# A grouped convolution in row tiles, on x in order of time

## What is computed

```python
def _L0_cond_ref(x, c, weight, c_weight, bias):   # 4 groups of 32 channels, 9 taps, padding 4
    out = lax.conv_general_dilated(x, weight, window_strides=(1,), padding=[(4, 4)],
              dimension_numbers=('NCH', 'OIH', 'NCH'), feature_group_count=4)
    return out + jnp.einsum('nd,od->no', c, c_weight)[:, :, None] + bias[None, :, None]

def _L1_cond_ref(x, embedding, W0, b0, W1, b1, W2, b2, weight, bias_k):
    h = gelu(embedding @ W0 + b0);  h = gelu(h @ W1 + b1)
    att = softmax(h @ W2 + b2)                              # 8 weights for each sample
    agg_w = jnp.einsum('bk,koi->boi', att, weight[..., 0])  # a 128x128 matrix for each sample
    return jnp.einsum('boi,bih->boh', agg_w, x) + (att @ bias_k)[:, :, None]

x = x + _L0_cond_ref(x, cond_128, ...)
x = x + _L1_cond_ref(x, cond_128, ...)
```

## Time and profile before

| | us |
|---|---|
| median of 3 runs | 840.06 |
| the profiled execution | 839.29 |
| its span, first to last instruction | 837.4 |
| TensorE busy in it | 766.2 |
| ACT busy | 637.2 |
| POOL busy | 552.1 |
| DVE busy | 410.1 |

### The profile page before, as it was taken

How to read it: one execution, slowest core, us unless ns; L and a number is a source line. 1 busy time by engine, 2 the same in 40 slices (tenths; PEclk the granted TensorE clock), 3 DMA queues, 4 the chain that set the end, 5 groups by cost and what they waited for, 6 DMA issues and landing times.

```text
span 837.4 us, 15303 instructions
## 1 busy us (share of the span) xinstructions
PE 766.2 (92%) x5424; PEld 600.9 (72%) x5424; DVE 410.1 (49%) x299; ACT 637.2 (76%) x291; POOL 552.1 (66%) x596
## 2 busy tenths in 40 slices
PE   2659998999999999999999999999999999999994
PEld 2547776777777777777777777777777777777773
DVE  6662455445445555444555445445554444554430
ACT  7766886888778877878786787888777868866554
POOL 3289686667778767767876666668667566866620
PEclk9988999999999999999999999999999999999997
DMA  5778999999999999999999999999999999987643
GB/s 194 206 230 263 309 317 292 305 326 306 325 314 330 313 313 308 318 301 306 329 318 306 297 312 312 319 331 332 305 314 300 284 305 327 319 257 247 220 164 126
DMA packets 91011, 242.90 MB, mean 290 GB/s; under 512 B 15914, under 2 KB 58482, under 8 KB 74610
## 3 DMA queue, kind: packets, MB, share of 16 engines
q1 hardware_dynamic: 90994, 242.67, 91.5%
HBM read 101.57 MB, written 75.50 MB: 211 GB/s over the span
## 4 chain that ended last, share of the span: by engine, by line
SPq 46%; PE 20%; DMA 20%; ACT 6%; issue 6%; POOL 1%; DVE 0%; POOLq 0%
SPq L240 34%; DMA mix_dram<-mix_parts 16%; PE ps L366 12%; SPq L264 9%; PE ps L383 8%; DMA mix_rep<-mix_dram 3%; ACT z_out L448 3%; SPq L272 2%; ACT x_ph L429 1%; ACT x_cv L452 1%; DMA x_in<-in_x_dram 1%; ACT z_out L452 0%; SPq L214 0%; PE ps L353 0%; POOL mix_prod L646 0%
## 5 line engine op out<-in xcount | busy, mean ns | idle before, releaser
L448 ACT ACTIVATE z_out<-ps,par 128x2048 f32<-128x2048 f32 x64 | 253.3, 3957 | 143.0 <-PE ps L383 143.0
L515 DVE TENSOR_TENSOR y_lo<-ps,y_hi 128x1024 fp32r<-128x1024 f32 x128 | 156.4, 1222 | 305.9 <-ACT y_hi L438 305.9
L429 ACT ACTIVATE x_ph<-x_in 128x2048 f32<-128x2048 f32 x63 | 246.5, 3914 | 0.0
L366 PE MATMUL ps<-x_hi,cw_hi 128*128 128x512 f32 x768 | 228.6, 406 | 0.3 <-DVE y_lo L515 0.3
L366 PE MATMUL ps<-x_hi,cw_lo 128*128 128x512 f32 x768 | 221.3, 397 | 0.0
L366 PE MATMUL ps<-x_lo,cw_hi 128*128 128x512 f32 x768 | 220.2, 395 | 0.0
L383 PE MATMUL ps<-y_hi,mix_rep 32*128 32x512 f32 x2048 | 179.7, 418 | 41.2 <-DMA mix_rep<-mix_dram 32.8
L366 PEld LDWEIGHTS ps<-x_hi,cw_hi 128*128 128x128 f32 x768 | 141.1, 191 | 52.2 <-issue 15.0
L366 PEld LDWEIGHTS ps<-x_hi,cw_lo 128*128 128x128 f32 x768 | 145.9, 190 | 33.9
L366 PEld LDWEIGHTS ps<-x_lo,cw_hi 128*128 128x128 f32 x768 | 145.4, 189 | 33.7
L438 ACT ACTIVATE y_hi<-ps 128x1024 fp32r<-128x1024 f32 x128 | 131.0, 1023 | 47.3 <-PE ps L366 47.3
(11 more groups left out here) (69 smaller groups left out, 87.8 us busy)
## 6 DMA issues: line engine op xcount, KB each, us to landing
x_in<-in_x_dram SPq DMA_DIRECT2D x64, 1024.0 KB, 6.2
out_dram<-z_out SPq DMA_DIRECT2D x64, 1024.0 KB, 5.9
x_cv<-x_ph SPq DMA_DIRECT2D x496, 128.0 KB, 3.8
mix_rep<-mix_dram SPq DMA_DIRECT2D x256, 128.0 KB, 4.0
mix_dram<-mix_parts SPq DMA_DIRECT2D x64, 128.0 KB, 2.7
mixw_nat<-in_L_cond_weight_dram SPq DMA_DIRECT2D x1, 512.0 KB
x_cv<-x_ph SPq DMA_DIRECT2D x8, 64.0 KB, 4.2
z_out<-in_L_cond_weight_dram SPq DMA_DIRECT2D x1, 144.0 KB, 2.2
```

The source lines that it names most:

```text
L366: mm = pe.matmul(y_ps[:, g, :], w[:, g, b, :], xx[buf(s)][:, g, b:b + N], start=n == 0, stop=n == len(terms) - 1)
L429: nc.scalar.activation(x_ph[pair_buf(s)][:, :, buf(s), :], x_in[buf(s)][:, :].rearrange("c (n q) -> c q n", q=PH), ACT.Copy).then_inc(x_sp ...
L448: nc.scalar.activation(z_out[buf(s)][:, :].rearrange("c (n q) -> c q n", q=PH), z_ps[:, :, :], ACT.Identity, bias=par[s[1]][:, NK:NK + 1]) ...
L515: nc.vector.tensor_tensor(y_lo[buf(s)][:, y_halves[h], :], y_ps[:, y_halves[h], :], y_hi[buf(s)][:, y_halves[h], :].bitcast(F32), ALU.subt ...
```

## The change

The convolution also runs in row tiles. Tile g is group g: its 32 rows are the group's 32 channels, as x lies in SBUF anyway, and its 128 weight columns are again 4 phases by 32 outputs. There are 12 offsets in time (`M`), nine taps for each of four phases, so a tile makes 12 by 3 terms = 36 matmuls (`CONV`), and a round of four tiles takes the place of one matmul of 128 rows. The moving operand for offset m is column n's point 4n+m: TensorE reads every fourth element of `x_hi` or `x_lo`, a step of 16 bytes. `x_ph`, `x_cv`, `split_phases` and `move_x` are gone; DVE splits `x_in` directly.

The tiles are staggered: tile t is `LAG` = 4 steps behind tile t-1. A slot has 48 steps, 36 of the convolution and 12 of the previous sample's mix. ACT and DVE take y bank by bank, ACT takes z two banks at a time, reading the two banks in turn and writing pairs of neighbours. The loads run 3 samples ahead (7 before), SP's order in a slot is load, store_mix, store, load_mix, and the small network's matmuls stand between the first sample's steps. The identity that adds x to the convolution is now added to the taps by a matmul.

```diff
+        def x_at(tile, rows, m):
+            return tile[rows, :].rearrange("p (n q) -> p n q", q=PH)[:, m // PH:m // PH + N, m % PH]
...
-            def conv(s):
...
-                        mm = pe.matmul(y_ps[:, g, :], w[:, g, b, :], xx[buf(s)][:, g, b:b + N],
-                                       start=n == 0, stop=n == len(terms) - 1)
...
+            between = {4: (turn_cond,), 10: (first_layer, turn_mixw), 20: (second_layer,), 28: (third_layer,),
+                       32: (context_mixed,), 44: (attention,)}
+            def conv_step(s, g, i):
...
+                rows = slice(Q * g, Q * g + Q)
+                if i == 0:
+                    if g == 0:
+                        pe.wait_ge(x_lo_made, done(s))
+                    at_least(pe, y_lo_made, done(s, G, lag=-2) + g + 1)
+                m, term = i // 3, i % 3
+                w, xx = ((cw_hi, x_hi), (cw_lo, x_hi), (cw_hi, x_lo))[term]
+                mm = pe.matmul(y_ps[:, g, :], w[rows, m, :], x_at(xx[buf(s)], rows, m),
+                               start=i == 0, stop=i == CONV - 1)
...
             def slot(s):
-                conv(s)
-                mix(after(s, -1))
+                for i in range(STEPS):
...
+                    for t in range(PH):
+                        if i >= LAG * t:
+                            step(s, t, i - LAG * t)
+                        else:
+                            step(after(s, -1), t, i - LAG * t + STEPS)
...
-            def take_z(s):
+            def take_z(s, h):
...
+                pair = slice(2 * h, 2 * h + 2)
+                nc.scalar.activation(z_out[buf(s)][:, :].rearrange("c (n q) -> c n q", q=PH)[:, :, pair], z_ps[:, pair, :].rearrange("c q n -> c n q"),
+                                     ACT.Identity, bias=par[s[1]][:, NK:NK + 1]).then_inc(z_read, 1)
...
             def slot(s):
-                if is_sample(s, 0):
-                    finish_table()
-                else:
-                    split_x(after(s, 1))
-                rest_y(s, 0)
-                rest_y(s, 1)
+                if not is_sample(s, 0):
+                    round_x(after(s, 1))
+                    rest_x(after(s, 1))
+                for g in range(G):
+                    rest_y(s, g)
```

More of the change, by code:

```diff
@@ L83, in cond_resid_kernel, with x_inner, x_halo @@
         x_in = two(sb, "x_in", [P, T])
[L84 to L87, removed]
+        x_hi = two(sb, "x_hi", [P, T + 2 * PH], F32R)
+        x_lo = two(sb, "x_lo", [P, T + 2 * PH], F32R)
+        def x_inner(tile):
+            return tile[:, PH:PH + T]
+        def x_halo(tile):
+            return tile[:, :].rearrange("p (n q) -> p n q", q=PH)[:, 0:N + 2:N + 1, :]
+        def x_at(tile, rows, m):
+            return tile[rows, :].rearrange("p (n q) -> p n q", q=PH)[:, m // PH:m // PH + N, m % PH]
         y_hi = two(sb, "y_hi", [P, G, N], F32R)
@@ L219, in load @@
                     return
-                b, split = ahead(number(s), done(s, lag=-2))
-                at_least(sp, x_split_ph, split)
+                b, taken = ahead(number(s), done(s, lag=-2))
+                at_least(sp, x_lo_made, taken)
                 sp.dma_start(x_in[buf(s)][:, :], x[b, :, :]).then_inc(x_loaded[buf(s)], DMA)
[L225 to L241, removed]
             def store_mix(s):
@@ L332, in _ @@
[L332 to L344, removed]
+                mm = pe.matmul(ps[:, k // 4, k % 4 * P:k % 4 * P + P],
+                               cw_rep[:, k, :, :].rearrange("o q c -> o (q c)"), ident[:, :],
+                               start=True, stop=k != K // 2)
@@ new lines, in first_layer, with turn_mixw @@
+            def first_layer():
+                pe.wait_ge(cond_copied, 3)
+                pe.matmul(ps[:, 5, 0:NS], w0_sb[:, :], cond_t[:, :], start=True, stop=True).then_inc(mlp_mm, 1)
+                pe.matmul(ps[:, 4, 0:NS], ctxw_t[:, :], cond_t[:, :], start=True, stop=True).then_inc(ctx_mm, 1)
+            def turn_mixw():
+                for k in range(NK):
+                    mm = pe.transpose(ps[:, 6 + k // 4, k % 4 * P:k % 4 * P + P], mixw_nat[:, k, :], ident[:, :])
+                mm.then_inc(mixw_turned, 1)
@@ L346, in attention, with context_mixed @@
+            def context_mixed():
+                pe.wait_ge(mixw_copied, 1)
+                pe.wait_ge(ctx_made, 1)
+                for k in range(NK):
+                    mm = pe.matmul(ps[:, 6, k * NS:(k + 1) * NS], mixw_t[:, k, :], ctx_c[:, :], start=True, stop=True)
+                mm.then_inc(ctx_mix_mm, 1)
             def attention():
@@ L368, in conv, with mix_step @@
                     mm.then_inc(y_ready, 1)
-                    if is_sample(s, 0) and g == 2:
-                        attention()
-            def mix(s):
+            def mix_step(s, r, i):
                 if not exists(s):
                     return
[L375 to L385, removed]
@@ new lines, in mix_step, with step @@
+                mm = pe.matmul(z_ps[:, r, :], mix_rep[buf(s)][rows, g, h, :], yy[buf(s)][rows, g, :],
+                               start=i == 0, stop=i == MIX - 1)
+                if i == MIX - 1:
+                    mm.then_inc(z_ready, 1)
+            def step(s, t, i):
+                if i < CONV:
+                    conv_step(s, t, i)
+                else:
+                    mix_step(after(s, -1), t, i - CONV)
+            def slot(s):
+                for i in range(STEPS):
+                    if is_sample(s, 0) and i in between:
+                        for part in between[i]:
+                            part()
+                    for t in range(PH):
+                        if i >= LAG * t:
+                            step(s, t, i - LAG * t)
+                        else:
+                            step(after(s, -1), t, i - LAG * t + STEPS)
@@ L412, in move_x0 @@
-        def move_x0(eng, groups, copy, moved):
-            eng.wait_ge(x_loaded[0], DMA)
             for g in groups:
-                for p in range(PH):
-                    n = copy(x_cv[0][Q * p:Q * p + Q, g, 0, :],
-                             x_in[0][Q * g:Q * g + Q, :].rearrange("c (n q) -> c q n", q=PH)[:, p, :])
-            n.then_inc(moved, 1)
+                rows = slice(Q * g, Q * g + Q)
+                write(wt_f[rows, :, :], wt_ps[rows, 0:K, Q * g:Q * g + Q]).then_inc(wt_copied, 1)
```

331 lines of the change are left out of this document (138 added, 193 removed).

## The result

The changed kernel takes 1286.76 us (1286.5 to 1289.35, 4 runs) against 839.76 us (836.22 to 840.33, 4 runs): 1.534 times the time of before, 95% interval 1.530 to 1.539. The profiled execution has a span of 1284.7 us.

What follows compares the result with a forecast made beforehand. TensorE was taken as the floor, SP's queue a little above it. Start 62 + 61 x 11.04 + end 28.5 = 764, with 3 for uneven rounds and 1.9 outside the span: 769, so 770 us; range 745 to 1470, the forecast's own 748 to 790.

Steps and rivals of the forecast that it cites:

- The step that failed: TensorE's convolution: a round of four stepped matmuls costs 0.230 us, as the mix's; 0.46 kept as the upper bound.
- the start: Time until sample 2's first convolution matmul: 62 us, bounds 52 to 67, against 67.46 before.
- the end: From sample 63's first matmul to the span's end: 28.5 us against 29.3, z in halves being about 1 us sooner.
- My two arguments against it: Against a halved TensorE read: its SBUF path is at least twice as wide as ACT's; POOL's step costs only 10%.
- The seams: TensorE's two changes per sample between full-array and row-tiled matmuls: 0.49 us a sample goes, 30 us in all.
- the waits: TensorE's waits, seen for the sample's matrix from DRAM: 0.61 us a sample goes, 37 us in all.
- PSUM, ACT and DVE: Freeing y's banks within 2.76 us and ACT's and DVE's work per sample: all fit the slot, costed at nothing.
- Rival A: The step halves TensorE's reads, slowing all 48 rounds to 0.46 us: 1460 us, or 1360 at 0.427; chance 0.34.
- B: Four times the instructions hold TensorE's pace: 0.25 to 0.40 us a round, 830 to 1270 us; chance 0.09.
- C: The matrix chain (POOL, two DRAM hops) becomes the bound: 11.5 to 12.1 us a sample, 800 to 835; chance 0.06.

Runs made afterwards that it cites:

- the run with neighbours: The changed kernel with each convolution matmul reading 512 neighbouring elements instead of every fourth, so other values: 765.95 us.
- the run with z alone: The kernel before, with only ACT's z in two halves that read two banks in turn and write pairs: 834.75 us, 0.995 of before.
- the first repair: The changed kernel with x_hi and x_lo laid out by phase, so TensorE reads neighbours and ACT and DVE take the step: 806.09 us, 0.960 of before.

## Why the prediction was wrong

The step that failed is the one that I singled out, "I take 0.230, the row of the same engine and the same form, and keep 0.46 as the other end": with the step a round of the convolution takes 0.461 us. Against the run with neighbours that is (19.36 - 11.12) x 61 = 503 us between sample 2 and sample 63, and 18 more at the start (sample 2 at 70.0 us instead of 61.6) and the end (33.9 us instead of 24.2). The row I took agreed in engine, shape and tiling, and differed in the one thing that the change was about. ACT's copy with a step, a factor of 2.05, agreed in that thing and gave 0.47. My two arguments against it did not bear on the question: a path twice as wide can be halved as well, and POOL, which takes 1252 ns for 512 elements without a step, where ACT takes 626, says nothing on an engine that reads faster.

- The rest of the sum held, except the end. Without the step the kernel takes 766 us where I had 770: a sample 11.12 us (11.04 and 0.05 forecast), sample 2 at 61.6 us (62, though its parts were off by 2 us each way: first convolution at 16.8 and not 15, first mix at 57.2 and not 59), the end 24.2 us (28.5). I had z in halves 1 us sooner at the end; the run with z alone shows 4, as the last two z's both stand in that chain.
- The seams and the waits are gone as said: in the run with neighbours the stretch of 200 us has TensorE busy for 200.00, and of 11.12 us a sample only 0.08 are not 48 x 0.230.
- PSUM, ACT and DVE: y a bank 597 and 692 ns (0.6 and 0.69 forecast), z 1230 ns for a half, between the bounds. The 12 rounds between two convolutions on a bank were time enough, as forecast; without the stagger they are not, for 31 us.
- Rival A had the mechanism, with 1460 us; measured 1287. "in the stagger no round is free of convolution (...), and the queue is in order, so all 48 rounds go at the slow pace" is wrong: the tiles are streams of their own, 19.36 us a sample and not 22.1, which is 167 us; the mix's matmuls stayed at their pace, where I had expected them as slow as their neighbours. The other 6 us are the end, 33.9 and not 40. B, the number of instructions, and C, the matrix chain, did not occur in the changed kernel; the late matrix of C came with the first repair, at 11.67 us a sample.
- The rule of the Trainium skill (SBUF — State Buffer, Specifications (TRN2)) pointed the right way for the step of four. That two hits in a line are enough is not borne out for this operand: a step of two has them, and so have the runs of four that start 8 bytes into a line, and both cost double; here it takes all four elements of a line. The other rule of the Trainium skill, that a change of tiling mode drains the engine (TensorEngine Tiling (Array Packing), Key Properties), agrees again, as the 0.49 us at the seams are gone with the changes of mode.

What was not tried is what the step costs ACT at 8 bytes, and another data type on TensorE, so the reading in slots holds for float32r alone.

## What to carry to other kernels

When a change alters how an operand is read, price it by a row that reads that way, even of another engine, before one that only looks alike; and a cost that no row of the engine shows deserves the first experiment, here one line. Lay a float32r moving operand out so that TensorE reads whole 16-byte lines, and let an engine with time to spare take the step: ACT took it for 3.9 us a sample and the kernel went from 840 to 773 us. After such a move, look again at what waits in SP's queue behind the slower engine: it was 34 us here.

## What the hardware showed beyond that

- Four row tiles are four streams, each with its own pace: matmuls of one tile started every 0.23 us beside others at 0.46, ahead of their order in the program.
- ACT reading two PSUM banks in turn and writing pairs takes 1180 to 1230 ns for 1024 elements, against 3957 for 2048 read bank by bank and written with a step of 16 bytes. Which of the two changes does it was not tried.
- DVE's tensor_tensor with one stepped input of 2048 elements takes 3887 ns, against 2437 without the step.
- Row-tiled matmuls with their weight loads hold 58 ns each from sample 2 to the last (11.12 us for 192, run with neighbours).
